# A two-layer decoder on one core: keys, queries and values of 768 of 1024 rows made beside the recurrence and fetched from DRAM by self attention

## What is computed

```python
x = _layernorm(x + _L0_attn_ref(x, ...), axis=-1)      # a recurrence over the 1024 rows
x = _layernorm(x + _L0_xattn_ref(x, ctx, ...), axis=-1)
x = _layernorm(x + _L0_ffn_ref(x, ...), axis=-1)
x = _layernorm(x + _L1_attn_ref(x, ...), axis=-1)      # self attention
...
def step(S, inp):                                      # the recurrence, four blocks of 32x32
    retrieved = jnp.einsum('bnij,bnj->bni', S, kn)
    S_upd = jnp.tanh(beta_t[..., None] * S + outer)
    S_new = (1.0 - w) * S + w * S_upd
...
def _L1_attn_ref(X, W_qkv, W_out):                     # 16 heads of 64
    qkv = X @ W_qkv
    qkv = qkv.reshape(b, s, h, d, 3)
    q, k, v = (qkv[..., 0], qkv[..., 1], qkv[..., 2])
    scores = jnp.einsum('bqhd,bkhd->bhqk', q, k) / scale
    weights = jax.nn.softmax(scores, axis=-1)
    attn = jnp.einsum('bhqk,bkhd->bqhd', weights, v)
```

## Time and profile before

| | us |
|---|---|
| median of 3 runs | 2861.58 |
| lowest and highest | 2861.42, 2862.21 |
| the profiled execution | 2855.75 |
| its span in the profile | 2854.0 |

### The profile page before, as it was taken

The page is one execution under the profiler, slowest core; times in us unless marked ns, Lnnn a source line. Parts: engine busy times, 40 slices in busy tenths (PEclk is TensorE's granted clock), DMA queues, the critical chain, the costliest instruction groups (busy, mean ns, idle before and its releaser), DMA issues. The chain is left out here.

```text
span 2854.0 us, 41502 instructions
## 1 busy us (share of the span) xinstructions
PE 2037.6 (71%) x11052; PEld 1151.4 (40%) x11052; DVE 2191.7 (77%) x10063; ACT 1747.8 (61%) x5698; POOL 653.7 (23%) x343
## 2 busy tenths in 40 slices
PE   6232555645556555564656699999999999699997
PEld 3222434434334443343434334333343333465554
DVE  5999999999999999999998455555555555276677
ACT  3678888888888888888882244444444444222231
POOL 0000000000000000000000267676676767100000
PEclk9555556555555555655556799999999999799999
DMA  4732232222222222222210000000000000201100
GB/s 120 151 100 49 49 71 53 55 49 62 62 53 55 55 64 55 53 55 65 59 33 5 4 13 18 9 16 17 15 13 13 15 13 12 89 8 45 41 12 8
DMA packets 86798, 123.55 MB, mean 43 GB/s; under 512 B 17444, under 2 KB 65224, under 8 KB 86600
## 3 DMA queue, kind: packets, MB, share of 16 engines
q1 hardware_dynamic: 86600, 121.37, 17.7%
HBM read 100.33 MB, written 21.00 MB: 43 GB/s over the span
## 5 line engine op out<-in xcount | busy, mean ns | idle before, releaser
L1507 ACT ACTIVATE mix_cand<-mix_pre,mixer_cbuf 128x32 f32<-128x32 f32 x2048 | 591.4, 289 | 164.9 <-DVE mix_pre L1434 81.8
L1504 ACT ACTIVATE mix_cand<-mix_state,mixer_cbuf 128x32 f32<-128x32 f32 x2048 | 653.0, 319 | 34.8 <-DVE mix_state L1426 4.7
L1421 DVE SCALAR_TENSOR_TENSOR mix_prod<-mixer_keys,mixer_cbuf,mix_cand 128x65 f32<-128x65 f32 x2048 | 578.8, 283 | 34.8 <-ACT mix_cand L1507 27.8
L1972 DVE TENSOR_REDUCE self_tops<-self_rough 128x2 f32<-128x1024 f32 x252 | 308.5, 1224 | 357.1 <-PE self_rough L1736 353.9
L1434 DVE SCALAR_TENSOR_TENSOR mix_pre<-mixer_keys,mix_gap,mix_state 128x32 f32<-128x32 f32 x2048 | 523.0, 255 | 27.7
L1537 PE MATMUL mix_out<-all_ident,mix_state 128*128 128x128 f32 x504 | 159.2, 416 | 484.2 <-ACT mix_flat L1488 428.8
L1426 DVE SCALAR_TENSOR_TENSOR mix_state<-mix_cand,mixer_cbuf 128x32 f32<-128x32 f32 x2048 | 503.5, 246 | 0.1
L1958 POOL TENSOR_TENSOR self_psum<-self_psum,self_prob 128x1024 f32<-128x1024 f32 x192 | 451.6, 2352 | 128.5 <-ACT self_prob L1885 118.9
L1885 ACT ACTIVATE self_prob<-self_sco 128x1024 f32<-128x1024 f32 x256 | 260.4, 1024 | 102.5 <-PE self_sco L1749 88.6
L875 POOL TENSOR_TENSOR mix_st_norm_rstd<-mix_st_norm_var,mix_half 128x2 f32<-128x2 f32 x24 | 17.4, 723 | 1300.6 <-DVE mix_st_norm_var L868 1300.6
L1537 PEld LDWEIGHTS mix_out<-all_ident,mix_state 128*128 128x128 f32 x504 | 81.2, 206 | 565.1 <-ACT mix_flat L1488 501.0
(11 more groups left out here) (397 smaller groups left out, 3260.9 us busy)
## 6 DMA issues: line engine op xcount, KB each, us to landing
mixer_keys<-k_rows SPq DMA_DIRECT2D x256, 260.0 KB, 4.9
aT_rows<-self_aT SPq DMA_DIRECT2D x32, 256.0 KB, 2.3
two_aT<-aT_rows SPq DMA_DIRECT2D x8, 1024.0 KB, 7.3
coef_rows<-mixer_coef SPq DMA_DIRECT2D x4, 1280.0 KB, 7.2
mixer_cbuf<-coef_rows SPq DMA_DIRECT2D x64, 80.0 KB, 5.6
k_rows<-mixer_krow SPq DMA_DIRECT2D x32, 65.0 KB, 4.7
proj_xin<-in_xT SPq DMA_DIRECT2D x8, 256.0 KB, 3.3
mix_st_xin<-in_x SPq DMA_DIRECT2D x8, 256.0 KB, 5.6
```

The lines of the kernel that those rows point to most:

```text
L1421: dve.scalar_tensor_tensor(prod[:, b, :], keys[:, h, b, s_, :], coef(NIB, h, s_, b), cand[:, b, s % 2, :], ALU.mult, ALU.mult, accum_out=g ...
L1504: act.activation(cand[:, b, (s + 1) % 2, NS:2 * NS], state[:, hp, sp_, b, :], ACT.Copy, scale=cbuf[:, h, KEEP, b, s_:s_ + 1]).then_inc(kep ...
L1507: act.activation(cand[:, b, (s + 1) % 2, 0:NS], pre[b], ACT.Tanh, scale=cbuf[:, h, BETA, b, s_:s_ + 1]).then_inc(c_ready[b], 1)
L1972: dve.tensor_reduce(tops[:, kh, t, :], of[:, :, :], AX.X, ALU.max).then_inc(rough_taken, 1)
```

## The change

Rows 0 to 767 (`EARLY`) get their keys, queries and values in `mix_layer`. A new class `EarlyRows` stands beside the steps of rounds 2 to 7, working on the rows of six rounds before: the copy at slot 141.5 now goes to `xT_now`, a tile of one round, and for each of the eight head pairs PE makes K, Q and V of the 128 rows of both batches (24 fills of 256 columns a round, 144 in all), ACT copies each to one of four slots of `row`, and SP stores it to `kq_rows` or `v_rows` in DRAM and loads the weights of the head pair after next. `WINDOWS` names bank, PE's slot and ACT's slot of each fill; at the end of a window PE waits for ACT's copies.

In `self_attention` a pair needs only the last 256 rows: one fill for K and Q together (four matmuls of 256 columns), one for V (four of 128). SP fetches the other 768 rows of K and Q (768 KB) and of V (384 KB) a pair ahead, and ACT casts the fetched K and Q to bf16 in two pieces (`cast_rows`). `shift` has two buffers, and the order of PE, ACT and DVE in a half is another one. The diff, cut:

```diff
+EARLY = T - 2 * ROUND
-        act.activation(self.xT_all[:, :, :, i * ROUND:(i + 1) * ROUND],
+        at = (i + 1) * ROUND - EARLY
+        act.activation(self.xT_last[:, :, :, at - ROUND:at] if at > 0 else self.xT_now[:, :, :, :],
+class EarlyRows:
+    N, SLOTS = 3 * PAIRS, 4
+    WINDOWS = ((33, ((2, 14.6, 17), (3, 16.6, 19), (2, 18.6, 21), (3, 20.6, 23), (2, 25.6, 28), (3, 27.6, 30), (2, 29.6, 33))),
+               (41, ((2, 35.2, 38),)),
+               (88, ((4, 74.6, 77), (3, 76.6, 79), (4, 78.6, 81), (3, 80.6, 83), (4, 83.6, 86))),
+               (114, ((2, 89.6, 92), (0, 91.6, 94), (2, 94.6, 97), (0, 96.6, 99), (2, 98.6, 101), (0, 100.6, 103), (2, 102.6, 105),
+                      (0, 104.6, 107), (2, 106.6, 109), (0, 108.6, 111), (2, 110.6, 113))))
+    def sp(self, sp, i):
...
+            yield place + 0.3
+            sp.wait_ge(self.taken, n + 1)
...
+            sp.dma_start(to, row).then_inc(self.stored[n % self.SLOTS], 16)
+            m = i * PAIRS + h
+            if c == 2 and m + 2 < EARLY // ROUND * PAIRS:
+                self.load(sp, m + 2)
+    def pe(self, pe, i):
...
+                yield place
+                if k == 0:
+                    pe.wait_ge(self.turned, i + 1)
+                if c == 0:
+                    pe.wait_ge(self.w_loaded[m % 2], 16 * (m // 2 + 1))
+                if n > 1:
+                    pe.wait_ge(self.taken, n - 1)
...
+            yield end
+            pe.wait_ge(self.taken, i * self.N + k)
+    def act(self, act, i):
+        for k, (bank, _, place) in enumerate(self.places):
+            n = i * self.N + k
+            yield place
+            act.wait_ge(self.made, n + 1)
+            if n >= self.SLOTS:
+                act.wait_ge(self.stored[n % self.SLOTS], 16 * (n // self.SLOTS))
+            act.activation(self.row[:, n % self.SLOTS, :], self.banks[bank][:, 0:B * ROUND], ACT.Copy).then_inc(self.taken, 1)
...
-    AHEAD = ("K0", "K1", "Q0", "Q1", "V0", "V1", "TOP0")
-    FILLS = ("K0", "DEN0", "K1", "TOP1", "Q0", "Q1", "DEN1", "V0", "TOP0", "V1")
+    AHEAD = ("KQ", "V", "TOP0")
+    FILLS = ("KQ", "DEN0", "V", "TOP1", "DEN1", "TOP0")
...
+            def moves(h, n, b, first, last):
+                fills = Fills(n, first, last)
+                if not last:
+                    of = (h, 1) if b == 0 else (h + 1, 0)
+                    if not first:
+                        wait_apart(sp, (setup, 1), s_ready, n * 2 * NQ)
+                    load_kq(*of)
+                    if not first:
+                        wait_apart(sp, (setup, 1), attended, n * NQ)
+                    load_v(*of)
+                if not first:
+                    store(h if b == 1 else h - 1, n - 1, 1 - b, 1)
+                if b == 0 and not (isinstance(h, int) and h == PAIRS - 1):
+                    wait_apart(sp, (setup, 1), made, fills.after("V"))
+                    load_w(h + 1)
                 store(h, n, b, 0)
...
+            def cast_rows(b, c, loaded):
+                if c == 0:
+                    act.wait_ge(kq_loaded[b], loaded)
+                act.activation(qkb[:, b, c, 0:EARLY], qk[:, b, c, 0:EARLY], ACT.Copy).then_inc(cast, 1)
```

More of the change, by code:

```diff
@@ L1397, in _ @@
                     load_x(i)
+            rows_out.until(T)
             store(NI - 2)
@@ L1513, in _ @@
                 beside.until(s)
+                rows.until(s)
             act.wait_ge(read_summed, NCH - 1)
@@ L1793, in pair @@
                 fills, other = Fills(n, first, last), 1 - b
-                pe.wait_ge(taken, fills.at if first else fills.at - 1)
                 for hf in range(2):
@@ L1800, in pair, with rough_next @@
                     of, to = (b, 1) if hf == 0 else (other, 0)
-                    if hf == 1:
-                        pe.wait_ge(taken, fills.after("TOP1"))
+                    def rough_next(r):
+                        if more:
+                            rough_scores(hp + 1, of, to, r)
+                    if hf == 1 and not last:
+                        pe.wait_ge(taken, fills.after("KQ"))
+                        pe.wait_ge(cast, n * 2 + 4)
+                    rough_next(0)
+                    pe.wait_ge(taken, fills.after("TOP1") if hf else fills.at)
@@ L1819, in pair @@
-                    if more:
-                        rough_scores(hp + 1, of, to, 2)
+                    if hf == 0 and not last:
+                        if b == 1:
+                            pe.wait_ge(w_loaded, n * 8 + 8)
+                        wait(pe, taken, fills.before("KQ"))
+                        keys_queries(other, misc[:, :])
+                    rough_next(2)
                     scores(hp, b, hf, 2)
                     scores(hp, b, hf, 3)
-                    if more:
-                        rough_scores(hp + 1, of, to, 3)
@@ L1838, in pair @@
-                    attend(hp, b, 1)
-                    if more:
-                        rough_scores(hp + 1, of, to, 6)
-                    if not last:
-                        if b == 1 and hf == 1:
-                            pe.wait_ge(v_loaded, n * 8 + 8)
-                        (values if hf else keys_queries)(fills, "V0" if hf else "K1", other)
-                    if more:
-                        rough_scores(hp + 1, of, to, 7)
+                    rough_next(4)
+                    if hf == 0:
+                        pe.wait_ge(v_loaded[b], n * 8 + (16 - 8 * b))
@@ L1849, in pair @@
+                    attend(hp, b, 0)
+                    rough_next(5)
+                    attend(hp, b, 1)
+                    rough_next(6)
+                    scores(hp, b, hf, 5)
+                    if hf == 0 and not last:
+                        wait(pe, taken, fills.before("V"))
+                        values(other, misc[:, :])
                     scores(hp, b, hf, 6)
-                    scores(hp, b, hf, 7)
+                    rough_next(7)
+                    attend(hp, b, 2)
@@ L1851, in pair @@
                     if more:
                         turn_tops(fills, "TOP0" if hf else "TOP1", hp + 1)
-                    attend(hp, b, 2)
-                    if not last:
-                        (values if hf else keys_queries)(fills, "V1" if hf else "Q0", other)
+                    scores(hp, b, hf, 7)
             each_pair(pe, pair)
@@ L1897, in _ @@
             ahead = Ahead()
-            for name, bank in zip(AHEAD, ahead_banks):
-                take(ahead, name, 0, bank)
+            take_rows(ahead, 0, ahead_banks[0])
+            take_values(ahead, 0, ahead_banks[1])
+            for c in range(2):
+                cast_rows(0, c, 16)
             def pair(n, b, first, last):
@@ L1905, in pair @@
                     fresh = first and hf == 0
+                    rows = hf == 0 and not last
                     weigh(hp, 0, fresh)
@@ L1909, in pair @@
                         take_out(hp - 1, 1 - hf)
-                    if not last:
-                        take(fills, "Q1" if hf else "K0", other)
+                    if rows:
+                        take_rows(fills, other)
                     weigh(hp, 2, fresh)
```

203 lines of the change are left out of this document (104 added, 99 removed).

## The result

Over four runs of each, the median goes from 2861.50 to 2780.37 us (2775.34 to 2786.26): a ratio of 0.9718, with a 95% interval of 0.9706 to 0.9729. That is 81 us gained where 147 were forecast, and the time lies above the range (2700 to 2768). The profiled execution is the longest of the four, 2786.26 us with a span of 2784.5, while the one of the kernel before lies 5.8 us under its median. So the two profiles are 69.5 us apart where the medians are 81.

What follows compares the result with a forecast made beforehand. DVE and ACT were taken to bound the steps, PE self attention. Terms -151.5 + 5 - 2.5 + 0 + 2 = -147 us gave 2708.75 for the profiled execution, 2714.5 as median; range 2700 to 2768.

Steps and rivals of the forecast that it cites:

- What bounds it: Steps are a loop between DVE and ACT with PE half idle; self attention is PE without a gap, 763.05 of 763.30 us.
- What comes back: Late fills in self attention: 0.94 us for four 256-column matmuls, 0.50 for V's four of 128, 1.44 us a pair.
- The second way to the number: Two pair-15 first halves without fills, 19.75 us of PE each, and 1.44 make 40.9 us, 10.1 less than 51.06.
- Handovers: Self attention's new order fits PE's pace by margins of tenths; 0.3 us a pair charged, +5 us (0 to 39).
- My walk: One half of a self-attention pair in the new order, followed with the old durations: all waits fit, by margins of tenths.
- A fill must not be late: Beside the steps, PE's slot is 2.4 steps (3.1 us) ahead of ACT's for a fill of 1.3 us: cost 0.
- ACT's copies: 144 copies beside the steps, 0.03 us charged for each of 60: +2 us (0 to 54).
- The rival by which they are paid in full: Beside the steps, ACT's copies cost 54 us instead of 2, giving 2766 us; chance 0.12.
- The fetches: Rows for self attention's next pair: 768 KB lands in 5 to 10 us, before it is needed; cost 0.
- the start: Start of self attention: 1 to 2 us gained, against PE idling and a later clock rise; set at 0 (-4 to +4).
- the last pair: Pair 15's first half in self attention gives back its waits: -2.5 us (0 to -2.6).
- slower: the copies wait: Late fills beside the steps stall both batches at each of 144 takes; at 1.5 us a fill 2929 us, chance 0.03.

Runs made afterwards that it cites:

- the fastest kernel: Changed kernel with the maxima joined by a one-source reduction and ten fills placed by what is queued on PE before them: 2738.75 us, ratio 0.9568.
- the last experiment but one: Changed kernel with the maxima joined by a one-source reduction, and half of each late fill's features left out in self attention: 2739.41 us, ratio 0.9571.
- the two experiments on it: Changed kernel with the maxima joined by a one-source reduction: 2762.19 us; changed kernel with POOL's work cut to 64 of 512 columns after the first pair: 2758.60 us.
- the kernel with one source: Changed kernel with the two halves of the maxima joined by one reduction over one source instead of a two-source maximum: 2762.19 us, ratio 0.9657.
- the run by queue: Changed kernel with ten fills, and copies of theirs, placed by what is queued on PE before them: 2759.08 us, ratio 0.9644.
- the second execution: The changed kernel run again without edits, for a second profile: 2781.85 us, ratio 0.9723 to the kernel before.

## Why the prediction was wrong

- **What bounds it** was right: 642.35 of 642.5 us of the pairs are PE's in the fastest kernel, and the last experiment but one moved both by the same 1.31 us.
- **What comes back: the first failed step.** I took four matmuls of 256 columns to be half of an "x8" in the earlier trace rows. The trace has two entries for each float32 matmul, so that "x8" is four of the program. The earlier trace rows said so too: the value fill, eight matmuls in the program, is "x16", and I divided its time by sixteen for each of "four". The fills cost 3.01 us a pair, not 1.44: 1.57 x 15 = 24 us. The second way to the number agreed only because it used the same 1.44.
- **Handovers: the second failed step.** My walk had "the transpose 0.4 us after the joined maxima", as if the join kept its 0.17 us of the trace before, where none overlapped POOL. It takes 1.03 us, a margin of 0.4 can't cover that, and a pair loses 44.33 - 42.96 = 1.37 us, 20.5 us in all, where I charged 0.3 a pair. The new order moved the join into POOL's instructions, and a duration that depends on its neighbours can't be carried over.
- The Trainium skill, "SBUF — State Buffer", SBUF: two separate sides, has that rule, and I didn't weigh it: a DVE operation with two SBUF inputs and a GpSimd one that reads SBUF take their common port as an exclusive lock, and the second waits for the whole instruction of the first. The joins that end 0.02 us after POOL's instruction agree, as do the two experiments on it.
- **The order's own price** was a term that I put at nothing. The corrected sum is 51.06 - 11.64 + 3.01 = 42.43 us a pair, and the kernel with one source needs 42.96. These 0.5 us are no waits that the profile shows: PE has no gap there (642.35 of 642.50 us in the fastest kernel). By distances of starts in one pair of it the score products (L1853) take 14.45 us where they took 13.95 before, and the others change by less and cancel. Seven of the 16 score tiles take 0.96 us instead of 0.86, where two did before, each time to the hundredth, which a short wait hidden under a modelled end would hardly do. That the 0.3 us charged for waits came near these 0.5 is luck. Both lengths stand in this view, one behind a rough tile and one behind a fill:
```profile
2072.98 1.02 PE L1853 MATMUL self_sco<-self_qk 64*128 64x512 f32 x4
2073.84 0.38 PE L1857 MATMUL self_sco<-self_shift,self_onesb 64*128 64x512 bf16 x2
2074.15 1.16 PE L1822 MATMUL self_misc<-keep_w_pair,keep_xT 128*128 128x128 f32 x8
2075.24 1.13 PE L1853 MATMUL self_sco<-self_qk 64*128 64x512 f32 x4
2076.20 0.38 PE L1857 MATMUL self_sco<-self_shift,self_onesb 64*128 64x512 bf16 x2
```
- **A fill must not be late: the third failed step.** I set 2.4 steps of lead against "a fill of 1.3 us". But a place in the table is where an instruction is put in the queue, not when PE gets there: fill 0, put at 14.6, started at 18.0, behind a `read_out` that waits for step 15's flip and takes 3.4 us. The fill itself takes 1.9 to 2.1 us at the half clock, and "1 to 1.3" has the same wrong count in it: a fill of K or Q is two matmuls and four entries, which start 0.43 us apart there. The late fills cost 20 to 25 us (the steps of the kernels with these places are 23 to 27.5 us longer than before, and 2.7 of that stay; the 1.6 us of steps 66 and 70 are in it up to twice), and the run by queue got 20.4 back. I also looked only at ACT's wait for `made`. Over a quarter of the new waits (5.9 of 21.5 us) were flips behind a late turn.
- **ACT's copies** were right: with the waits gone the steps take 1410.5 us, 2.7 over those before, where I had 2. Of the 2.7, 1.6 are steps 66 and 70 of a round at the half clock. The rival by which they are paid in full falls.
- **The fetches, the start and the last pair** were right: 4.8 us for 768 KB, -1.0 (-3.4 in the second execution), -2.3.
- The rival "slower: the copies wait" had the right mechanism and the wrong size: 21.5 us of new waits are 0.15 us a fill, where it had 1.5. They fall on three of 24 in the first profile: fills 0 and 13, which are late themselves, and fill 8, which makes a turn late.

The trace before already held the 24 us of the fills. For the queue it held `read_out`'s 3.6 us and the order around it, though the 20 us are what the runs measured. With both, the forecast would have been about 2759; the join's 20 us, which needed the rule on the shared port, bring it to 2779, and the measured median is 2780.

## What to carry to other kernels

Where an engine works in program order, the lead of an inserted instruction is the time from when the engine gets there, so look up what stands ahead of it and what that waits for, and then who waits for the instructions behind it. Moving the waiting copy alone left ACT waiting for the turn behind the same fill. Count entries of the trace against the matmuls of the program before a price is taken from a group. And when an order moves, look at which instructions of DVE and POOL will now overlap: an operation of two SBUF sources on a critical handover beside POOL was better written with one here, by 20 us.

## What the runs showed of the hardware

- A DVE `tensor_tensor` on 8 float32 elements, both sources in SBUF, takes 167 ns alone and 1033 in the median (2146 at most) when POOL runs `tensor_tensor`s of 1.27 and 2.35 us on SBUF, and 261 ns when POOL's take 0.45. A reduction with one source takes 174 ns at the same place, and a multiplication with one source in PSUM keeps its 0.69 us under POOL.
- Added work on PE raised its granted clock over the steps from 0.57 to 0.65 of the full one, and the same fills with 32 columns instead of 256 put it back to 0.57. `read_out` takes 3.4 us at 0.50 of the full clock and 1.8 at the full one.
- `second_layer` varies by up to 8 us between executions, and step 70 of a round by 1.22 us between rounds, each with the granted clock of that stretch. Left open: why the clock rises in one execution or round and not in another that runs the same instructions.
